# New turn lists for two interleaved streams in a Perceiver block on one core: cross attention, linear attention, experts

## The reference, cut to what matters

```python
# part 1, B=64: cross attention block
y = _layernorm(x); y = layernorm(y + attention(y, y, y, causal=True), g1, beta1)
y = layernorm(y + attention(y, ctx, ctx, causal=False), g2, beta2)
x = x + layernorm(y + relu(y @ w1 + b1) @ w2 + b2, g3, beta3)
# part 2, over the other axis (T=64 steps, B=32), L=2 layers, H=8 heads of 16
for l in range(2):
    h = rmsnorm(u, norm1_w[l])          # q, k, v, beta from h; delta rule over T:
    #   S += beta k (v - S k)^T ; o = S q
    u = u + rmsnorm(o) @ Wo[l]
    h = rmsnorm(u, norm2_w[l]); u = u + (silu(h @ Wg) * (h @ Wy)) @ Wd[l]
x = x + rmsnorm(u, final_norm_w)
# part 3: 32 experts (I=64), 8 chosen of 4 groups, and one shared expert
x = x + routed(layernorm(x)) + shared(layernorm(x))
```

## Time and profile before

| | us |
|---|---|
| median of 3 runs | 721.45 |
| lowest, highest | 720.89, 730.81 |
| the profiled execution | 717.71 |
| span of its trace | 715.9 |
| mean granted TensorE clock | 0.870 of full |

### The profile page before, as it was taken

How to read it: one execution, slowest core, us unless ns; L and a number is a source line. 1 busy time by engine, 2 the same in 40 slices (tenths; PEclk the granted TensorE clock), 3 DMA queues, 4 the chain that set the end, 5 groups by cost and what they waited for, 6 DMA issues and landing times.

```text
span 715.9 us, 17173 instructions
## 1 busy us (share of the span) xinstructions
PE 587.2 (82%) x7376; PEld 395.0 (55%) x7376; DVE 448.5 (63%) x1125; ACT 257.6 (36%) x571; POOL 96.9 (14%) x140
## 2 busy tenths in 40 slices
PE   1687980877799999796699769968689999999994
PEld 1544650467698867656498647854444444444442
DVE  4956495888868444847846972874665555555552
ACT  1365530654340635353434244243322222222221
POOL 2454471410000102100100010210200000000000
PEclk9988995875569999898758889997879999999998
DMA  9995003000000000000000410000212634344321
GB/s 333 320 369 222 1 20 99 0 2 2 2 2 5 4 2 2 2 2 1 1 3 4 136 55 2 5 1 1 66 30 66 173 88 112 85 105 114 88 60 29
DMA packets 19084, 46.78 MB, mean 65 GB/s; under 512 B 3809, under 2 KB 8545, under 8 KB 18753
## 3 DMA queue, kind: packets, MB, share of 16 engines
q1 hardware_dynamic: 18368, 45.43, 20.8%
q10 hardware_dynamic: 640, 0.26, 0.2%
HBM read 43.32 MB, written 2.36 MB: 64 GB/s over the span
## 4 chain that ended last, share of the span: by engine, by line
PE 60%; DVE 25%; ACT 4%; POOL 4%; SPq 2%; issue 2%; DMA 2%; DVEq 0%; POOLq 0%
PE psum L760 8%; PE psum L755 8%; PE psum L765 8%; PE psum L596 4%; PE psum L718 3%; PE psum L692 3%; PE psum L721 3%; PE psum L562 3%; PE psum L727 2%; POOL rstd L963 2%; SPq L410 2%; DVE yr L1302 2%; PE psum L623 2%; PE psum L466 2%; PE psum L681 2%
## 5 line engine op out<-in xcount | busy, mean ns | idle before, releaser
L942 ACT ACTIVATE arena<-psum 128x512 f32<-128x512 f32 x68 | 40.6, 597 | 133.3 <-PE psum L755 125.5
L1380 DVE TENSOR_TENSOR arena<-psum,arena 128x512 f32<-128x512 f32 x64 | 44.2, 691 | 62.2 <-PE psum L760 60.4
L765 PE MATMUL psum<-arena,wed_sb 128*128 128x512 f32 x128 | 67.0, 606 | 0.0
L783 ACT ACTIVATE arena<-psum 128x512 f32<-128x512 f32 (+1 forms) x72 | 34.3, 501 | 66.4 <-PE psum L562 40.8
L1385 DVE TENSOR_TENSOR arena<-arena 128x512 f32<-128x512 f32 x64 | 44.3, 692 | 14.7 <-PE psum L765 14.6
L562 PE MATMUL psum<-arena 32*64 32x128 f32 x1024 | 42.3, 322 | 9.9 <-DVE XA L1295 5.2
L562 PEld LDWEIGHTS psum<-arena 32*64 32x64 f32 x1024 | 36.2, 162 | 14.8 <-DVE XA L1295 5.9
L962 POOL TENSOR_TENSOR ve<-ss,eps_rms 128x4 f32<-128x4 f32 x16 | 4.3, 270 | 287.6 <-ACT yr L834 201.5
L765 PEld LDWEIGHTS psum<-arena,wed_sb 128*128 128x128 f32 x128 | 24.9, 194 | 31.6 <-issue 24.2
L760 PE MATMUL psum<-yT,weu_sb 128*128 128x512 f32 x68 | 37.3, 632 | 3.9 <-DVE arena L1380 3.9
L755 PE MATMUL psum<-yT,weg_sb 128*128 128x512 f32 x68 | 36.9, 626 | 2.2 <-ACT yr L783 2.2
(11 more groups left out here) (284 smaller groups left out, 1221.2 us busy)
## 6 DMA issues: line engine op xcount, KB each, us to landing
arena<-shares SPq DMA_DIRECT2D x64, 256.0 KB, 4.0
arena<-in_ctx_t SPq DMA_DIRECT2D x16, 514.0 KB, 8.4
arena<-in_ctx_z SPq DMA_DIRECT2D x16, 512.0 KB, 9.4
XA<-in_x SPq DMA_DIRECT2D x1, 1024.0 KB, 4.9
zlast<-in_ctx_last SPq DMA_DIRECT2D x4, 256.0 KB, 16.6
X<-x_mid SPq DMA_DIRECT2D x2, 512.0 KB, 4.5
weg_sb<-in_we_gate SPq DMA_DIRECT2D x2, 512.0 KB, 6.4
weu_sb<-in_we_up SPq DMA_DIRECT2D x2, 512.0 KB, 7.2
```

Of the source, the lines that this page charges most:

```text
L765: pe.matmul(x3, wed_sb[:, (p - 1) % (NPAIR + 1), :], act_a[pr], start=(p == 0), stop=False, skip_group_check=True).then_inc(x_down[pr], 1)
L783: return act.activation(out_, in_, ACT.Copy, scale=scale)
L942: act.activation(act_g[pr], banks[4 * pr + 2 * (n % 2)], ACT.Silu).then_inc(x_silu[pr], 1)
L1380: dve.tensor_tensor(act_gu[pr], banks[4 * pr + 1], act_g[pr], ALU.mult).then_inc(x_gu[pr], 1)
```

## The change

Two strings are replaced and nothing else: same steps, same instructions, same semaphores, same DMAs.

```diff
-XTURNS = "AABAABABBABAAAAAABABABABAABABBAABBBABBBABABBBB"
+XTURNS = "ABABAAAAAAAABABBABABBABAAABABBAABBBABBBAABBBBB"
-TURNS = ("AABAABAABAABBAABABABAABBAABAABABBAABAABBAAAAAAABBABABAABBABABAABABABAABAABABABBBABABABAABAABABAB"
-         "ABBABAAABBAABAABABABABABABABABABABABABAAABBBBBBBBBABAAABBABBABBBBBABABBBAABAAABAABABABBBABBAABBA"
-         "BBBABAABABBBAABABABAAABBBAABAABAABBBABABBBABBAABBBABAB")
+TURNS = ("AABABAABABBAABAAABABAABAABABABABBAABBABAAAAAAABABABABAABBBABAAAABBABABAAAABABAABABAABAABBBAABABABA"
+         "BBABBBAAABBABBABABAABABBBBABABABAABBBBABABABABABAABABBBAABBABABBBBAABABABBAABAAABAABAABABAABBBAABB"
+         "ABBBBAABAABABBBBAAABABABAAABABBBBABAABBABBBBBABBBABBB")
```

More of the change, by code:

```diff
@@ L86 @@
 ROUTE = ["eln", "etr", "elog", "ro0", "ro1", "ro2", "ec"]
-TURNS = ("AABAABAABAABBAABABABAABBAABAABABBAABAABBAAAAAAABBABABAABBABABAABABABAABAABABABBBABABABABAABAABAB"
-         "ABBABAAABBAABAABABABABABABABABABABABABAAABBBBBBBBBABAAABBABBABBBBBABABBBAABAAABAABABABBBABBAABBA"
-         "BBBABAABABBBAABABABAAABBBAABAABAABBBABABBBABBAABBBABAB")
+TURNS = ("AABABAABABBAABAAABABAABAABABABABBAABBABAAAAAAABABABABAABBBABAAAABBABABAAAABABAABABABAABBBAABABABA"
+         "BBABBBAAABBABBABABAABABBBBABABABAABBBBABABABABABAABABBAABBABABBBBAABABABBAABAAABAABAABABAABBBAABB"
+         "ABBBBAABAABABBBBAAABABABAAABABBBABAABBABBBBBABBBABBB")
 def cross_schedule():
```

## The result

The changed kernel takes 734.32 us in the median of 20 runs (724.51 to 744.53); before, run in turn with it on the same chips, takes 725.15 (717.03 to 731.02). The ratio is 1.0117, 95% interval 1.0078 to 1.0155: 8.5 us slower, less than 2%, but beyond what the measurement leaves open. The forecast was 720.0, range 711 to 732: too low by 14.3 us and outside its range. A ratio leaves out the executions more than 1.5% above the fastest of their kernel (such as the profiled one of e9_but_layer1, 773.28 us at a mean clock of 0.764), while medians count all (734.32 / 725.15 is 1.0126).

A forecast was written before the change was run, and what follows sets the result against it. PE bounds the experts and 205.8 to 290.4 us; DVE, PE and ACT chains bound most of the layers; order, the cross attention. Terms sum to -1.4 on 717.71, giving 716.3; the median 3.7 above gives 720.0, range 711 to 732.

The forecast's parts named there:

- cross attention: Cross attention: A.c5's maximum waits behind B.sas to B.sar, carrying a delay to part 1's end; loss of 7 us.
- layer 0: Layer 0: B's grams between A's inversion steps lose 1.5 us, A.down ahead of B.s2 gains 1.0; net 0.5 loss.
- layer 1: Layer 1: earlier A.gram0 and full clock in A.ah0 and A.ah1, partly given back later; gain of 4 us.
- routing: Routing: moving A.ro1 behind B.n2 leaves PE's wait before B.mtr as long as before; loss of 1 us.
- experts: Experts: two steps of A done before B.ro1 stops DVE, one stall left; gain of 4.5 us.
- tail: Tail: A's stores go out three steps earlier, so B's stores start sooner; gain of 1.4 us.
- A.x0 fills the 3.31 us: Start of the experts: A.x0 runs in the 3.31 us in which PE waited for B.eln.
- 1.3 + 1.2: Layer 0: B.gram0's 1.3 us between A.inv0 and A.inv1, plus two later grams waiting 0.6 us each, delay A.lout.
- A.down ahead of B.s2, 1.0 gained: Layer 0, behind A.lout: B's s and p steps cover A.n1/1's norm, a 1.19 us wait goes; 1.0 us gained.
- the 7 "shrink" to 4: Layer 1 after A.ah1: of the 7 us gained there, waits for B.kq and B's inversion leave 4.
- -4 becomes +3 if A.ah0 is at half rate and B.lout too: Layer 1, bound on its term: with both at half rate the gain of 4 us becomes a loss of 3.
- the second's (slower): Rival: cross attention's 7 us stand, layer 1 loses 3 at half rate; 727 us, decided at A.ah0/1's clock; chance 0.28.

The follow-up runs named there:

- e9_but_layer1: Whole change except turns 74 to 146 (layer 1), which keep the old order, against the kernel before: ratio 1.0086.
- e1_cross: Only the cross attention's order (XTURNS) new, TURNS old, against the kernel before: ratio 1.0150.
- e10_but_cross: All of TURNS new, the cross attention's order (XTURNS) old, against the kernel before: ratio 0.9961.
- e7_layer0_73: TURNS 1 to 73 new (layer 0 without the exchange of A.kq/1 and B.onorm/0), rest old, against the kernel before: ratio 1.0046.
- e12_layer1_second: Only TURNS 106 to 146 new (layer 1's second half, B.kq/1 to A.fin), against the kernel before: ratio 1.0116.
- e3_layer1: Only TURNS 78 to 146 new (layer 1 without the exchange of A.kq/1 and B.onorm/0), against the kernel before: ratio 1.0066.
- e8_layer1_73: Only TURNS 74 to 146 new (layer 1 with the exchange of A.kq/1 and B.onorm/0), against the kernel before: ratio 1.0104.
- e4_experts: Only TURNS from A.eln on new (147 to 246: routing, experts, tail), against the kernel before: ratio 0.9953.
- e11_layer1_first: Only TURNS 74 to 105 new (layer 1's first half, A.rs/1 to A.ah1/1), against the kernel before: ratio 0.9894.
- e16_second_inv: Only TURNS from B.ext/1 to 146 new: B.ext ahead of A.o, B's inversion without A's steps between, against the kernel before: ratio 1.0181.
- e5_front: Only XTURNS 1 to 7 new (B.st0 and B.nm0 ahead of A.sas), against the kernel before: ratio 0.9993.
- e13_two_gains: TURNS 74 to 105 and 147 to 246 new (layer 1's first half; routing, experts, tail), rest old, against the kernel before: ratio 0.9786.

## Why the prediction was wrong

Its steps against the shifts in the two profiled executions, and what the ratios say of each:

| step | predicted | between the traces | by ratio |
|---|---|---|---|
| cross attention | +7 | +6.5 | +10.9 alone, +11.4 in the change |
| layer 0 | +0.5 | +4.4 | +3.3 |
| layer 1 | -4 | -2.6 at B.o/1 | +4.8 (78 to 146) and +7.5 (74 to 146) alone; -7.7 and +8.4 by halves; +2 in the change |
| routing | +1 | +2.8 | not separable |
| experts | -4.5 | -1.4 | with the tail -7.8, with both -3.4 |
| tail | -1.4 | -2.9 | |
| sum | -1.4 | +6.8 | +8.5 |

In the traces the difference of 8.2 is layer 0 (3.9), the experts (3.1), routing (1.8) and layer 1 (1.4), less 1.5 of the tail and 0.5 of the cross attention. Three steps of the prediction failed: layer 0's term of 0.5, the price of layer 1's second half, and "A.x0 fills the 3.31 us" of the experts.

**Cross attention: right.** A.c0 at 33.86 (said 33.9), A.c3 at 37.73 (37.6), part 1 6.8 late (7). Behind A.c3 two errors partly cancelled: A.c5 came at 47.97 (said 49.2), since B.sar began at 42.7 and not at 44.0, and the way from there to B.c0 took 5.4 us (said 4.8), so that B.c0 at 53.4 is close to the 54.0 said in part by luck. A.cr0's L1142 took 1.14 us instead of 3.27 and moved nothing, as the prediction had it: its 2.1 us were no gain. The Trainium skill (SBUF — State Buffer, Who interferes with whom) says that a DVE instruction with two inputs in SBUF contends with a GpSimd one that reads SBUF. The rows agree: before, L1142 ran from 44.03 to 47.30 beside GpSimd's L969 and L970, and now GpSimd's begin at 50.84, behind it. What e1_cross's ratio shows above 7 is 1.5 us in layer 0, and 2.4 that no trace shows and neither the interval nor the medians need.

**Layer 0: the term was mis-sized, 0.5 for 3.3 to 4.4.** "1.3 + 1.2" was right in kind: B's evacuations and a wait between A's inversion steps, measured 2.04 at A.inv2. Two credits failed. "A.ext ends 1.0 earlier" came true only in e10_but_cross's trace; in e7_layer0_73's it was even, and in the changed kernel A.ext was 2.4 later: A.sq on ACT stands behind B.tr (1.2), and A.kt0 and A.gram0 ran at half clock behind the longer wait (1.98 us for 32 matmuls of A.gram0, 1.10 before). And "A.down ahead of B.s2, 1.0 gained": the shift was 10.95 at A.lout, 11.57 at A.onorm and 10.91 at the end of B.o, so it gave back 0.7 of what had just been lost. Beside that I had moved B.gram0 on DVE and not on PE: its 3.69 us ran under A.ext, where PE now waits 7.70, and now lie in the inversion.

**Layer 1: the sum of a right gain and a loss priced at a third.** Up to A.ah1 the prediction's steps came true in kind: counted from the end of layer 0, A.gram0 was 8.3 us early in the changed kernel (8 said), A.ext 10.3 (13 said) and A.ah1 6.5 (7.4 said), with A.ah0 and A.ah1 at full clock. The failed step is the next one, that the 7 "shrink" to 4 over the second half. That is a price of 3, and the second half measures 8.4 alone (e12_layer1_second). In the changed kernel's profiled execution the step looks nearly right: A.onorm 5.9 later (5.7 said), from there to the end of B.o 49.7 us (48.5 said), B.o 2.6 early (4 said), a price of 3.9. But that execution was a favourable one. In the traces of the three other kernels with this order of layer 1 the price from A.ah1's end on was 8.4 (e3_layer1), 14.5 (e8_layer1_73) and 12.0 us (e10_but_cross), and B.o/1 ended 5.4, 8.6 and 7.3 late. What took its place: half clock in B.lout, B.ah0 and A.wo (7.04, 7.04 and 3.78 in e3_layer1), and in e8_layer1_73 and e10_but_cross already in B's grams (clock 0.50 from 374 to 394 us, 1.00 in the changed kernel), beside the waits for B's inversion. The bound "-4 becomes +3 if A.ah0 is at half rate and B.lout too" tied the loss to the wrong place: A.ah0 was at full clock and the loss came all the same. What the full change pays for layer 1 is not settled: 2 us by leaving it out, 7.5 alone, 0.7 by the product of the halves. The trace of e8_layer1_73 shows how it varies: the lead of 10 us at A.ext was gone at B.ext, with half clock between them (B.gram0 3.84 us for 1.92, A.o 13.8), while the changed kernel's profiled execution kept full clock in B's grams and in most of A.o.

**Routing: 1 for 2.8.** A.fin and A.eln before B.onorm were said to cost 2.2 and cost 2.8: B.o ends 8.3 late, B.onorm 11.1. The prediction's sign, a wait of 7 or more before B.mtr, did not come: it was 4.47 us for 7.76, but A.etr (2.46) and B.otr (1.17) waited in its place, and all PE waits of the stretch were 8.2 us for 9.3. The loss may follow from layer 1's second half: e4_experts, which has the new routing without it, lost nothing there.

**Experts: the sign right, -4.5 for -1.4.** The failed step is "A.x0 fills the 3.31 us", which counted the wait as gone. B.eln was itself 1.4 later, 2.33 us stayed in front of B.etr, A.x3 waits 0.94, and A.x5 3.54 as said. All PE waits of the stretch together fell from 9.75 to 9.39. **Tail: -1.4 for -2.9**: I had left B's store the cost of standing near A's; it starts with its product.

**From the profile to the median.** I took the median 3.7 above the profiled execution, from 3 runs. Over 20 it was 7.4, and 9.8 for the changed kernel. So of the 14.3 us, 8.2 are the steps, 3.7 the median of before, and 2.4 that the changed kernel's median lies further from its profiled execution.

**The rivals.** The direction was the second's (slower), but not its mechanism: its deciding point, the clock at A.ah0, came out against it. The cross attention's 7 us standing with little given back is the part of it that held, and B.lout at half clock; the measured 734 lies beyond its 727.

## What to carry to other kernels

Two in-order streams pay where a step of one stands in a stretch in which the other has a chain: price each moved step on every engine that it has work on, PE too, and ask what filled the place that it leaves. Here an order that gathered one stream's chain emptied PE beside it and piled the other's work behind; it paid where the emptied time was short (A's grams, e11_layer1_first) and not where it was a whole inversion (e12_layer1_second and e16_second_inv). That is one kernel, and no general rule. And a large reordering can be a sum of gains and losses of the same size: cut it at the points where both lists have taken the same steps and measure the pieces, since the best kernel here (0.9786) is a part of a change that lost.

## What the runs showed that I had not expected

The clock is part of the variation, not only of the mean. At the end of layer 1, with the old order, B.o took 3.9 us a group in some traces and 7.0 in others (e5_front, e11_layer1_first, e13_two_gains): a swing of 6 us on one list, in a chain whose waits on PE before it are 0.15 to 0.42 us in the kernel before. The Trainium skill (TensorE: Matmul & The Clock Gate, Part 1) says that activity releases a throttled default. The rows agree where PE had waited (B.lin behind 7.80 us and B.lout behind 4.08 at half clock), but not at A.lout and A.ah0 of layer 0: 14 us of matmuls without a gap stayed at half clock in every trace (7.04 and 7.02 us). The same shapes do run at full clock elsewhere, A.lout/1 in 3.92 us, though they don't keep it surely: before, A.ah0/1 began at a clock of 1.00 behind a wait of 1.33 us and was at 0.50 within 1 us. What decides between the two isn't shown here.

Two moves that cost 10.9 and 13.1 us alone cost 8.4 together, and the two pieces of the cross attention's order gave 1.0039 where the whole gave 1.0150: single pieces need not add up, in either direction.
